# Taking the row maxima of both side banks with one VectorE operation in a cross-attention and mixture-of-experts kernel

## The reference, cut to what matters

```python
q = (layernorm(x) @ Wq)            # 16 batches, 256 tokens, 16 heads of 64
k, v = context @ Wk, context @ Wv  # 1601 rows for each batch
sim  = einsum('bhid,bhjd->bhij', q, k) * SCALE
attn = softmax(sim, axis=-1)
x    = x + (einsum('bhij,bhjd->bhid', attn, v)) @ Wo + bo
x    = x + moe(layernorm(x))       # 32 experts, 4 of them per token, and a shared one
```

## Time and profile before

| | |
|---|---|
| median of three executions | 3527.07 us |
| span of the profiled execution | 3526.0 us |
| loop over 64 groups | about 78 to 3073 us of the span, 46.8 us a group |
| TensorE busy | 3420.7 us (97%) |
| VectorE busy | 2504.7 us (71%) |
| ScalarE busy | 2027.4 us (57%) |
| GpSimd busy | 1163.2 us (33%) |

### The profile page before, as it was taken

The page is one execution under the profiler, slowest core; times in us unless marked ns, Lnnn a source line. Parts: engine busy times, 40 slices in busy tenths (PEclk is TensorE's granted clock), DMA queues, the critical chain, the costliest instruction groups (busy, mean ns, idle before and its releaser), DMA issues.

```text
span 3526.0 us, 54934 instructions
## 1 busy us (share of the span) xinstructions
PE 3420.7 (97%) x15929; PEld 2666.3 (76%) x15929; DVE 2504.7 (71%) x4705; ACT 2027.4 (57%) x2452; POOL 1163.2 (33%) x953
## 2 busy tenths in 40 slices
PE   6999999999999999999999999999999999979888
PEld 4777777777777777777777777777777777766665
DVE  5776776776776777677767767677767766778887
ACT  3566666565556665655566665665666666544443
POOL 3333332333333332323333323333333323324444
PEclk9999999999999999999999999999999999979999
DMA  2000000000000000000000000000000000020000
GB/s 67 0 0 8 0 8 0 8 0 8 0 8 0 8 0 8 0 8 0 1 7 0 8 0 8 0 8 0 8 0 8 0 8 0 1 38 6 6 6 6
DMA packets 18022, 22.31 MB, mean 6 GB/s; under 512 B 2976, under 2 KB 14280, under 8 KB 17928
## 3 DMA queue, kind: packets, MB, share of 16 engines
q1 hardware_dynamic: 17928, 20.86, 2.2%
HBM read 18.49 MB, written 2.10 MB: 6 GB/s over the span
## 4 chain that ended last, share of the span: by engine, by line
PE 83%; issue 8%; POOL 5%; DVE 2%; ACT 1%; DMA 0%; DVEq 0%; POOLq 0%; SPq 0%; ACTq 0%
PE side L577 12%; PE op L620 11%; PE op L622 11%; PE op L621 11%; PE st L609 10%; PE st L610 10%; PE st L611 10%; POOL h_lo L503 5%; PE side L630 3%; DVE cT_lo L1006 1%; PE side L526 1%; PE side L569 1%; ACT cT_hi L806 1%; PE side L571 1%; PE side L570 1%
## 5 line engine op out<-in xcount | busy, mean ns | idle before, releaser
L1031 DVE TENSOR_REDUCE m_part<-side 128x1 f32<-128x402 f32 x2064 | 1104.9, 571 | 518.8 <-PE side L577 510.4
L868 ACT ACTIVATE p_full<-st 128x1024 f32<-128x1024 f32 (+1 forms) x832 | 855.7, 1028 | 918.8 <-PE st L611 918.8
L282 POOL TENSOR_TENSOR p_lo<-p_full,p_hi 128x1024 fp32r<-128x1024 f32 x256 | 657.5, 2568 | 1064.5 <-ACT p_hi L871 1064.5
L282 DVE TENSOR_TENSOR p_lo<-p_full,p_hi 128x1024 fp32r<-128x1024 f32 (+1 forms) x576 | 717.6, 1246 | 222.7 <-ACT p_hi L871 222.7
L871 ACT ACTIVATE p_hi<-st 128x1024 fp32r<-128x1024 f32 (+1 forms) x832 | 853.1, 1025 | 0.0
L609 PE MATMUL st<-qT_hi,cT_hi 97*128 (+3 forms) x1668 | 677.2, 406 | 0.5 <-DMA qT_hi<-m_row 0.2
L610 PE MATMUL st<-qT_lo,cT_hi 96*128 (+3 forms) x1668 | 661.8, 397 | 0.0
L620 PE MATMUL op<-p_hi,v_hi 128*97 128x512 f32 (+1 forms) x1664 | 661.3, 397 | 0.0
L611 PE MATMUL st<-qT_hi,cT_lo 96*128 (+3 forms) x1668 | 659.0, 395 | 0.0
L622 PE MATMUL op<-p_hi,v_lo 128*97 128x512 f32 (+1 forms) x1664 | 656.1, 394 | 0.0
L621 PE MATMUL op<-p_lo,v_hi 128*97 128x512 f32 (+1 forms) x1664 | 655.5, 394 | 0.0
(11 more groups left out here) (182 smaller groups left out, 3241.1 us busy)
## 6 DMA issues: line engine op xcount, KB each, us to landing
nat<-in_ctx SPq DMA_DIRECT2D x18, 576.0 KB
out_x<-x SPq DMA_DIRECT2D x8, 256.0 KB, 2.3
qT_hi<-m_row SPq DMA_DIRECT2D x65, 4.0 KB
w_nat<-in_L_ffn_gate_w SPq DMA_DIRECT2D x2, 512.0 KB, 6.9
w_nat<-in_L_ffn_up_w SPq DMA_DIRECT2D x2, 512.0 KB, 9.5
Wq_sb<-in_L_xattn_Wq SPq DMA_DIRECT2D x1, 512.0 KB, 6.0
Wo_sb<-in_L_xattn_Wo SPq DMA_DIRECT2D x1, 512.0 KB, 9.0
nat<-in_ctx SPq DMA_DIRECT2D x18, 24.4 KB
```

The source lines that it names most:

```text
L282: eng.tensor_tensor(p_lo[0:m, slot(s), :], p_full[0:m, s % 2, :], p_hi[0:m, slot(s), :].bitcast(F32), ALU.subtract).then_inc(s_lo_pool if ...
L868: act.activation(p_full[0:m, s % 2, :], both(st[0:m, s % 2]), ACT.Exp, scale=SCALE)
L1031: dve.tensor_reduce(m_part[:, k:k + 1], where[:, 0:MAXW], AX.X, ALU.max).then_inc(s_drain, 1)
```

## The change

Each pair of M now fills both side banks with matmuls of the same tile of queries and two parts of the keys (`max_at`), and VectorE reduces both banks with one operation over 128 x 2 x 402 elements, which writes two columns of `m_part`. It waits for the second of the pair and raises `s_drain` by two at its end. So that every half slot holds a whole pair, `SLOTS` is written anew: slots 2 and 3 gain an M each in their second half, slots 5 and 8 lose the M ahead of C and Y. The pass ahead of the loop is changed in the same way.

```diff
-        SLOTS = {2: ("MM", "M"), 3: ("MM", "M"), 4: ("MM", "MM"), 5: ("MM", "MC"), 6: ("MM", "MM"),
-                 7: ("MM", "MM"), 8: ("MM", "MY"), 9: ("MM", "MM"), 10: ("MM", "MM"), 11: ("YY", "YT"),
+        SLOTS = {2: ("MM", "MM"), 3: ("MM", "MM"), 4: ("MM", "MM"), 5: ("MM", "C"), 6: ("MM", "MM"),
+                 7: ("MM", "MM"), 8: ("MM", "Y"), 9: ("MM", "MM"), 10: ("MM", "MM"), 11: ("YY", "YT"),
                  12: ("", "QQ")}
+
+        def max_at(k):
+
+            half, pair, part = k // (NM // 2), k // 2 % (NM // 4), k % 2
+            return pair, half * 2 + part
...
             def max_scores(where, k, par):
 
-                tile, part = k % (NM // 4), k // (NM // 4)
+                tile, part = max_at(k)
...
-            def reduce_max(where, filled, k):
+            def reduce_two(both_banks, filled, k):
+
                 dve.wait_ge(s_fill, filled)
-                k = k % (NM // 4) * 4 + k // (NM // 4)
-                dve.tensor_reduce(m_part[:, k:k + 1], where[:, 0:MAXW], AX.X, ALU.max).then_inc(s_drain, 1)
+                tile, part = max_at(k)
+                dve.tensor_reduce(m_part[:, tile * 4 + part:tile * 4 + part + 2], both_banks[:, :, 0:MAXW], AX.X,
+                                  ALU.max).then_inc(s_drain, 2)
...
-            for k in range(NM):
-                reduce_max(max_ps[k % 4], J0_M + k + 1, k)
+            for k in range(0, NM, 2):
+                reduce_two((side, op)[k // 2 % 2], J0_M + k + 2, k)
...
                         if kind == "M":
-                            reduce_max(bank(j), filled, k)
+                            if k % 2:
+                                reduce_two(side, filled, k - 1)
```

## The result

The changed kernel takes 3605.43 us (median of four, 3604.44 to 3606.33) against 3527.13 us for the kernel before; the ratio is 1.0221, 95% interval 1.0209 to 1.0232. It is 78 us slower. The prediction said slower, 3571 us, with a range up to 3604. The direction held, and the stalls after a `p_lo` came in the slots where they were forecast. The size was too small by 34 us, and one of the signs that the prediction had named for being wrong came true: half slots without a `p_lo` stall too.

A forecast was written before the change was run, and what follows sets the result against it. TensorE, busy 97%, was taken to bound the kernel. Stalls of 0.23 + 0.23 + 0.22 - 0.20 + 0.23 = +0.71 us a group, 45.4 us for 64 groups, less 0.7 ahead of the loop, gave 3571 us, range 3546 to 3604.

The forecast's parts named there:

- the stalls after a `p_lo`: New TensorE stalls at slots 3, 4 and 10, where a `p_lo` stands between two pairs: 0.23 us each per group.
- one of the signs that the prediction had named for being wrong: In the changed trace, a half slot without `p_lo` stalls; the prediction said this would show it wrong.
- slot 6, behind C: Slot 6's second M waits for `cT_lo` as before; the change adds 0.
- slot 8, behind the long `p_lo`: After slot 7's `p_lo` of 1.52 us, slot 8 stalls 0.53 us against 0.31 before, +0.22 a group.
- slot 9, behind Y: Without the M ahead of Y, the reciprocal begins 0.25 us sooner and slot 9's stall goes: -0.20 us a group.
- ahead of C, Y and T: C finds its bank just in time; moving C and Y and the waits of T cost nothing.
- VectorE starts 0.04 later: The merged reduction starts 0.04 us after the pair's two matmuls end, at 0.57 us from the pair's start.
- a plain half slot still fits: Without `p_lo`, the next M is possible at 1.71 us, wanted at 1.75 to 1.77: no stall, 0.05 us to spare.
- The price of the merged operation: Reduction of 804 elements on VectorE: 1.04 ns an element plus 0.15 us fixed, 0.99 us, bounds 0.84 and 1.06.
- The range: 3546 to 3604 us: merged operation between 0.94 and 1.04 us gives 3546 to 3597, stall readings some 7 more.
- The first: Rival: chip treats the merged operation as two, 1.06 us; eleven plain half slots miss by 0.02, 3621 us; chance 0.06.
- the rival for no change: Rival: merging saves the whole fixed 0.15 us of a pair, operation 0.91 us, kernel 3530 to 3531 us; chance 0.08.

The follow-up runs named there:

- one_up: The changed kernel, but the merged reduction raises `s_drain` by one and all waits count a pair as one; 3576.95 us, ratio 1.0143.
- flat: The changed kernel, but the merged reduction reads 804 contiguous elements across both banks and writes one column, still raising by two; 3607.08 us, ratio 1.023.
- late_pair: The changed kernel with two single reductions instead of the merged one, both after the second matmul, the second raising by two; 3618.97 us, ratio 1.0259.
- both_moved: As c_moved, and GpSimd makes A_lo and x_lo after its `p_lo` of tile 7 instead of tile 5; 3492.41 us, ratio 0.9902.
- c_moved: New slots with single, separately released reductions; slot 5 is M, M, M, C and slot 6's first half has one M; 3494.05 us, ratio 0.9906.

## Why the prediction fell short

The first column is what the prediction said for a group; the others are the extra distances of matmul starts, averaged over the groups of each trace. The prediction read the old stalls from one group (0.31 us at slot 8 and 0.20 at slot 9).

| stall, us a group | predicted | kernel before | raise by one | changed kernel |
|---|---|---|---|---|
| slots 3, 4 and 10, each | 0.23 | 0 | 0.22 to 0.23 | 0.26 to 0.27 |
| slot 6, behind C | 0.32, as before | 0.32 | 0.32 | 0.32 |
| slot 8, behind the long `p_lo` | 0.53 | 0.27 | 0.38 | 0.28 |
| slot 9, behind Y | 0 | 0.19 | 0 | 0 |
| nine plain pairs together | 0 | 0 | 0 | 0.28 |
| ahead of C, Y and T | 0 | 0 | 0.11 | 0.26 |

- **The step that failed** is "VectorE starts 0.04 later": a distance taken from the old instruction, whose wait rode in it. With a raise by two the wait stands alone, and the distance is 0.11. The steps that rested on 0.05 us to spare fell with it: nine pairs miss by 0.02 to 0.04 each, C, Y and slot 11 also, and the stalls at slots 3, 4 and 10 grow by 0.03 to 0.05. That "a plain half slot still fits" thus turned out false, and the nine pairs that miss are the sign of being wrong that the prediction named. `one_up` undoes just this and comes to 3577, 6 us from the 3571 predicted.
- **The price of the merged operation**, 0.99 us, was right (994 ns), and two rows cost nothing (`flat`). But its working joined a reduction of 402 elements out of PSUM with one of 32 elements out of `m_part`, which lies in SBUF. That both carry the same fixed part was taken without a row. The reductions out of PSUM alone, 571 ns for 402 and 994 ns for 804, give 0.15 us and 1.05 ns an element, so it made no difference.
- **The stalls after a `p_lo`** are there at the slots named. With the wait inside the reduction they are 0.22 to 0.23 us.
- **Slot 8** was priced too high. I took the 1.52 us of `p_lo` from one group of the old trace (the mean over the groups is 1.49) and called it fixed. It depended on GpSimd's x_lo, and when TensorE slows, this `p_lo` slides off it: a mean of 1.36 us in `one_up`, 1.23 in the changed kernel. This hid 0.25 us a group of the other error, 16 us in all. That the forecast missed by no more than 34 us is partly luck.
- **Slot 9's gain** came as worked out: no load waits for the addition.
- **Y's own loads** were missed: behind a reduction that ends just in time, the second of Y's short matmuls waits for its load (0.07 us in `one_up`).
- **The range**: the term that failed wasn't in it. It took the operation's length as unknown, which was known well, and the distance from a matmul's end to VectorE's start as known, for an instruction whose wait and raise had another form.
- **The rivals**: none came true. The first had the plain half slots miss by 0.02 us, which they do, but for an operation of 1.06 us, and it lasts 0.99. The Trainium skill's rule (VectorE: DVE Perf Modes, the section on the TRN2 errata), that one large operation pays the SBUF latency once, was the rival for no change. The trace bears it out only in part: the merge takes 0.07 us off a pair (1.06 to 0.99), not the whole fixed 0.15. The merge does save: 42 us from `late_pair` to `one_up`. But it saves against a pair that starts late, not against the kernel before, where the first reduction ran beside the second matmul.

## What to carry to other kernels

Merging two operations on an engine that has time to spare delays what they release: count when each buffer comes free, not how long the engine works. Where the waiting engine's slack is 0.05 us, check that the new instruction carries its wait and its raise in the same form; raising by two instead of one cost 28 us here. New slot orders are worth running alone: here they were a gain, hidden under the loss.

## What the runs showed of the hardware

- A reduction that waits on one semaphore and raises another by two has its wait issued as an instruction of its own, and starts 0.07 us later (0.11 against 0.04) when VectorE is idle. There are 1040 of them: 1024 in the loop wait for a register's value, and 16 ahead of it for a fixed number. Behind a busy VectorE nothing of it shows: after a `p_lo` the reduction starts 0.08 us before the end of its record, raised by two or by one.
- Reductions out of PSUM took 0.15 us and 1.05 ns an element (571 ns for 402, 994 for 804); 128 x 2 x 402 over two banks and 804 in a row both took 0.99 us.
- Where `p_lo` on VectorE and GpSimd's x_lo overlap, the one that started later is held up most. Alone `p_lo` takes 1.21 us (`both_moved`). It took 1.49 on average when it started 0.33 us after x_lo (the kernel before), 1.36 at 0.46 us (`one_up`) and 1.23 at 0.59 us (the changed kernel), while x_lo kept its 0.74. With `p_lo` first by 0.17 us (`c_moved`) it took 1.29, and x_lo 1.71. What the two share was not tested.
